# Routed block with 64 experts on one core: a fourth place for the down matrices, and three late shared tiles instead of four

## What is computed

```python
logits = xf @ w_router.T
top_vals, top_idx = jax.lax.top_k(logits, K)
w_tok = jax.nn.softmax(top_vals.astype(jnp.float32), axis=-1)
...
x_ec = xf[tok_ec]                                   # 64 experts x 64 places
g = jax.nn.silu(jnp.einsum('ech,ehi->eci', x_ec, w_gate))
u = jnp.einsum('ech,ehi->eci', x_ec, w_up)
y = jnp.einsum('eci,eih->ech', g * u, w_down)
contrib = (y * w_ec[..., None]).reshape(-1, h)
combined = jnp.zeros_like(xf).at[tok_ec.reshape(-1)].add(contrib)
combined = combined + silu(xf @ w_sh_gate) * (xf @ w_sh_up) @ w_sh_down
```

## Time and profile before

| | us |
|---|---|
| median of 3 runs | 703.38 (702.91 to 703.41) |
| the profiled execution | 701.8 |
| its span, first to last instruction | 699.9 |
| PE busy in the span | 661.4 (94%) |
| DVE, ACT, POOL busy | 316.3, 162.2, 220.5 |
| DMA packets | 203.17 MB, mean 290 GB/s over the span |

### The profile page before, as it was taken

How to read it: one execution, slowest core, us unless ns; L and a number is a source line. 1 busy time by engine, 2 the same in 40 slices (tenths; PEclk the granted TensorE clock), 3 DMA queues, 4 the chain that set the end, 5 groups by cost and what they waited for, 6 DMA issues and landing times.

```text
span 699.9 us, 8785 instructions
## 1 busy us (share of the span) xinstructions
PE 661.4 (94%) x3165; PEld 390.3 (56%) x3165; DVE 316.3 (45%) x750; ACT 162.2 (23%) x267; POOL 220.5 (32%) x209
## 2 busy tenths in 40 slices
PE   4999999999999898999999999999999999999873
PEld 3687878888878654444444444454454454444331
DVE  6887567759968771332332322233232222323111
ACT  5922215623211411121211211111121111112110
POOL 5537446446648131021222112221220203221011
PEclk9999999999999999999999999999999999999998
DMA  8201016713785979599999999999999999999993
GB/s 319 79 23 38 1 31 198 271 58 119 273 307 195 358 260 351 197 367 388 387 405 404 387 370 387 390 400 399 359 398 393 403 357 398 390 398 394 371 344 46
DMA packets 53195, 203.17 MB, mean 290 GB/s; under 512 B 7829, under 2 KB 8213, under 8 KB 52768
## 3 DMA queue, kind: packets, MB, share of 16 engines
q1 hardware_dynamic: 37360, 169.80, 61.3%
q0 software_dynamic: 8928, 21.26, 12.7%
q10 hardware_dynamic: 6864, 11.54, 4.4%
HBM read 179.21 MB, written 23.60 MB: 290 GB/s over the span
## 4 chain that ended last, share of the span: by engine, by line
PE 79%; DVE 5%; DMA 4%; issue 2%; ACT 1%; POOL 1%; POOLq 0%; SPq 0%; ACTq 0%; DVEq 0%
PE bank L1609 23%; PE bank L1394 13%; PE bank L1630 11%; PE bank L1527 9%; PE bank L1546 5%; PE bank L1416 4%; DMA extra<-in_L_ffn_w_up 3%; PE bank L1554 2%; PE bank L1441 2%; PE bank L1617 2%; PE bank L1539 1%; PE bank L1431 1%; PE bank L1583 1%; DVE key L1096 1%; PE bank L1363 1%
## 5 line engine op out<-in xcount | busy, mean ns | idle before, releaser
L652 POOL DMA_INDIRECT out_dram<-ym,midx x32 | 51.3, 1602 | 298.5 <-DVE ym L1260 107.1
L1609 PE MATMUL bank<-w_sb,xT 128*64 128x384 f32 x768 | 131.2, 494 | 2.8 <-issue 2.0
L1394 PE MATMUL bank<-x_hi,w_parts 128*128 128x512 f32 x368 | 114.9, 394 | 2.7 <-DVE x_lo L991 2.2
L1609 PEld LDWEIGHTS bank<-w_sb,xT 128*64 128x64 f32 x768 | 53.5, 138 | 74.3 <-issue 69.9
L1630 PE MATMUL bank<-w_sb,guT 128*64 128x512 f32 x384 | 88.0, 593 | 4.4 <-issue 4.4
L1394 PEld LDWEIGHTS bank<-x_hi,w_parts 128*128 128x128 f32 x368 | 69.6, 190 | 18.5 <-DVE x_lo L991 3.0
L1195 DVE TENSOR_TENSOR gu<-sg,bank 128x384 f32<-128x384 f32 x32 | 17.7, 555 | 126.1 <-PE bank L1609 65.2
L1394 PE MATMUL bank<-x_lo,w_parts 128*128 128x512 f32 x184 | 70.9, 394 | 0.0
L1527 PE MATMUL bank<-sh_sb,xS 128*128 128x384 f32 x192 | 63.9, 486 | 0.0
L1630 PEld LDWEIGHTS bank<-w_sb,guT 128*64 128x64 f32 x384 | 27.7, 137 | 53.3 <-issue 52.6
L1527 PEld LDWEIGHTS bank<-sh_sb,xS 128*128 128x128 f32 x192 | 35.7, 191 | 22.3
(11 more groups left out here) (187 smaller groups left out, 917.8 us busy)
## 6 DMA issues: line engine op xcount, KB each, us to landing
w_sb<-in_L_ffn_w_down SPq DMA_DIRECT2D x64, 768.0 KB
w_sb<-in_L_ffn_w_gate SPq DMA_DIRECT2D x48, 768.0 KB
w_sb<-in_L_ffn_w_up SPq DMA_DIRECT2D x48, 768.0 KB
extra<-in_L_ffn_w_gate SPq DMA_DIRECT2D x16, 768.0 KB
extra<-in_L_ffn_w_up SPq DMA_DIRECT2D x16, 768.0 KB
ring<-in_L_attn_x SPq DMA_DIRECT2D x14, 256.0 KB, 3.9
xt_dram<-xwT ACTq DMA_DIRECT2D x12, 256.0 KB, 2.9
xS<-xt_dram SPq DMA_DIRECT2D x12, 256.0 KB
```

Source lines behind the costliest of these rows:

```text
L652: pool.indirect_dma_start(out=out[:, :], out_offset=bass.IndirectOffsetOnAxis(ap=midx[j % 3][u][:, :], axis=0), in_=ym[u][:, :], in_offset ...
L1394: ins = pe.matmul(ps[u][:, :], w, xp, start=(n == 0), stop=(n == len(parts) - 1))
L1609: ins = pe.matmul(ps[e * C:(e + 1) * C, 0:I], xT[:, c, e * C:(e + 1) * C], gate_up(2 * j + u, e, k)[:, c, :], start=(c == 0), stop=(c == K ...
```

## The change

`place` is p mod 4 for all three kinds of matrix, so the down matrices have four places too. The room for the fourth comes from writing the gated rows over `sg` (no `gu` tiles any more; ACT's silu now waits for the transposes of the rows ahead instead of for their product), from moving `yS` onto the residual rows of the late tiles, and from moving `ym1` and `last_tok`. `load_down(p)` waits for the down product four pairs earlier, and SP's order becomes gate of p, up of p, down of p - 1; the down matrices of pair 3 are loaded ahead of group 0, one expert's right behind gate and up of pair 3, the other's after the late products. LEAD is 3 and FIRST is 1: three late tiles, all made ahead of group 0; group 0 has no shared product (it keeps the down product of the third late tile), and 13 tiles run in the groups 1 to 13. Tile 12 is therefore stored to DRAM by ACT, both as residual and transposed, ahead of group 0. BATCHES becomes 3, 6, 9, 12 and 13, the last with one tile. Ahead of group 0 the transposes of the third late tile go before the down product of the second.

```diff
-LEAD = 4
+LEAD = 3
 TAIL = 3
...
-FIRST = 2
+FIRST = 1
...
-            return p % (SLOTS + 1 if k < 2 else SLOTS)
+            return p % (SLOTS + 1)
...
-        BATCHES = range(FIRST + 2, FIRST + SHARED, 3)
+        BATCHES = [*range(FIRST + 2, FIRST + SHARED, 3), FIRST + SHARED - 1]
+
+        def batch(j):
+            last = j - FIRST
+            return last // 3 * 3, last + 1
...
             def load_down(p):
 
-                sp.wait_ge(d_ready[(p - SLOTS) % 2], (p - SLOTS) // 2 + 1)
+                sp.wait_ge(d_ready[p % 2], p // 2 - 1)
                 fill_matrix(sp, p, 2)
...
             fill_matrix(sp, 3, 0)
-            sp.wait_ge(u_ready[2], 1)
             fill_matrix(sp, 3, 1, (1,))
+            fill_matrix(sp, 3, 2, (1,))
             sp.wait_ge(half_ready, 1)
...
             fill_matrix(sp, 3, 1, (0,))
+            sp.wait_ge(u_ready[2], LEAD)
+            fill_matrix(sp, 3, 2, (0,))
             for p in range(4, 2 * GROUPS):
-                if p > 4:
-                    load_down(p - 2)
                 if p % 2 and 2 <= (p - 1) // 2 - FIRST < SHARED:
                     load_shared_tile((p - 1) // 2 - FIRST)
                 for k in range(2):
                     load_matrix(p, k)
-            load_down(2 * GROUPS - 2)
+                if p > 4:
+                    load_down(p - 1)
             load_down(2 * GROUPS - 1)
...
-                    pool.dma_start(out[(j - FIRST - 2) * P:(j - FIRST + 1) * P, :].rearrange("(a p) m -> p a m", p=P),
-                                   yS[:, :, :], accum_op=ALU.add).then_inc(added, ADD)
+                    t0, t1 = batch(j)
+                    pool.dma_start(out[t0 * P:t1 * P, :].rearrange("(a p) m -> p a m", p=P),
+                                   yS[:, 0:t1 - t0, :], accum_op=ALU.add).then_inc(added, ADD)
...
             def shared_out(t):
 
                 act.wait_ge(d_ready[2], t + LEAD + 1)
+                if t == 0:
+                    act.wait_ge(late_stored, 16 * LEAD)
...
-                dve.tensor_tensor(gu[0][:, :], sg[0][:, :], ps_u[0][:, 0:I], ALU.mult).then_inc(gu_ready[u], 1)
+                dve.tensor_tensor(sg[0][:, :], sg[0][:, :], ps_u[0][:, 0:I], ALU.mult).then_inc(gu_ready[u], 1)
...
             late_product(2, 1)
+            turn_shared(2, ps_xt)
             down_shared(1)
-            turn_shared(2, ps_xt)
...
                     down_shared(TAIL - 1)
-                    for w in range(2):
-                        late_product(TAIL, w)
```

More of the change, by code:

```diff
@@ L191, in moe_block @@
         assert 4 * ROW * 4 + W * 4 + 2 * 2048 <= 2 * KC * D * 4 + 2 * D * 4
-        sg, gu = ([tile(f"{name}{n}", [P, I], at=None if n < 1 else xw_at + i * I * 4) for n in range(2)]
-                  for i, name in enumerate(("sg", "gu")))
+        sg = [tile(f"sg{n}", [P, I], at=None if n < 1 else xw_at) for n in range(2)]
         guT = [tile(f"guT{n}", [P, IC, P], at=None if n < 1 else st_at + 2048) for n in range(2)]
         y, y_low = tile("y", [P, D], F32R, at=ramp_at), tile("y_low", [P, D], F32R, at=logits_at)
-        ym = [tile(f"ym{u}", [P, D]) for u in range(2)]
+        ym = [tile(f"ym{u}", [P, D], at=None if u < 1 else xw_at + I * 4) for u in range(2)]
         same = [tile(f"same{u}", [P, P], F32R) for u in range(2)]
@@ L201, in moe_block @@
         other_tok = [tile(f"other_tok{i}", [P, n * C], F16, at=a)
[L202 to L208, removed]
+                     for i, (n, a) in enumerate(((16, key_at), (8, wo_at + 2 * KC * D * 4 + 2 * D * 4 - 1024), (8, xw_at + I * 4 + 2048)))]
+        last_tok = tile("last_tok", [P, P], F16, at=st_at + 2048 + I * 4)
+        late_at = inv_at + (LATE - TILES) * 2048
+        yS = tile("yS", [P, 3, D], at=late_at)
+        assert st_at == vx_at + K4 and late_at + 3 * 2048 == out_at
+        extra_at = late_at - 2 * W * 4
+        assert top[0] <= extra_at - W * 4
+        assert 16 * C * 2 <= (HALF + C) * 4
         extra = [[tile(f"extra{k}{e}", [P, W], at=a) for e, a in enumerate(places)]
-                 for k, places in enumerate(((extra_at, extra_at + W * 4), (xin_at, wo_at + 4 * ROW * 4)))]
+                 for k, places in enumerate(((extra_at, extra_at + W * 4), (xin_at, wo_at + 4 * ROW * 4), (vx_at, extra_at - W * 4)))]
         assert W * 4 <= 3 * 2048
@@ L218, in place @@
         def place(p, k):
-            return p % (SLOTS + 1 if k < 2 else SLOTS)
+            return p % (SLOTS + 1)
         def uses(p, k):
-            return p // (SLOTS + 1 if k < 2 else SLOTS)
+            return p // (SLOTS + 1)
         def matrix(p, e, k):
@@ L234, in has_shared @@
         def has_shared(j):
-            return j == 0 or FIRST <= j < FIRST + SHARED
+            return FIRST <= j < FIRST + SHARED
         def item(j):
-            return LEAD + j - FIRST if j else TAIL
+            return LEAD + j - FIRST
         def in_parts(j, u):
@@ L333, in moe_block @@
         tok_ready, tok_turned, idx_ready = sem("tok_ready"), sem("tok_turned"), sem("idx_ready")
-        w_full = [[sem(f"w_full{k}_{i}") for i in range(SLOTS + (k < 2))] for k in range(3)]
+        w_full = [[sem(f"w_full{k}_{i}") for i in range(SLOTS + 1)] for k in range(3)]
         xg_full = [sem2(f"xg_full{r}") for r in range(2)]
@@ L882, in silu @@
                 act.wait_ge(g_ready[u], j + 1)
-                need(act, gu_ready[1 - u], j + u)
+                need(act, gu_turned[1 - u], j + u)
                 act.activation(sg[0][:, :], ps_g[0][:, 0:I], ACT.Silu).then_inc(sg_ready[u], 1)
@@ L887, in silu_shared @@
                 act.wait_ge(g_ready[2], t + 1)
-                need(act, gu_ready[2], t)
+                need(act, gu_turned[2], t)
                 act.activation(sg[1][:, :], ps_g[1][:, 0:I], ACT.Silu).then_inc(sg_ready[2], 1)
@@ L921, in group @@
                     pair_out(j, 1)
-                if first:
-                    store_late(TAIL)
-                elif shared:
+                if shared:
                     shared_out(j - FIRST)
@@ L1205, in gated_shared @@
                 need(dve, gu_turned[2], t)
-                dve.tensor_tensor(gu[1][:, :], sg[1][:, :], ps_u[1][:, 0:I], ALU.mult).then_inc(gu_ready[2], 1)
+                dve.tensor_tensor(sg[1][:, :], sg[1][:, :], ps_u[1][:, 0:I], ALU.mult).then_inc(gu_ready[2], 1)
             def turn_copy_shared(t):
@@ L1319, in group @@
                 merged_out(j, 0)
-                if first:
-                    shared_residual(TAIL)
                 same_tokens(j, 1)
@@ L1538, in turn_shared @@
                 for c in range(IC):
-                    ins = pe.transpose(ps[:, c * P:(c + 1) * P], chunk(gu[1][:, :], c, IC), ident[:, :])
+                    ins = pe.transpose(ps[:, c * P:(c + 1) * P], chunk(sg[1][:, :], c, IC), ident[:, :])
                 ins.then_inc(gu_turned[2], 1)
@@ L1616, in turn_gated @@
                 for c in range(IC):
-                    ins = pe.transpose(ps_ht[:, c * P:(c + 1) * P], chunk(gu[0][:, :], c, IC), ident[:, :])
+                    ins = pe.transpose(ps_ht[:, c * P:(c + 1) * P], chunk(sg[0][:, :], c, IC), ident[:, :])
                 ins.then_inc(gu_turned[u], 1)
```

## The result

| | before | changed |
|---|---|---|
| median of runs, us | 703.14 | 696.51 (696.30 to 696.61) |
| ratio, 95% interval | | 0.9908 (0.9896 to 0.9921) |
| profiled execution, us | 701.8 | 696.56 |
| its span, us | 699.9 | 694.7 |

The kernel is faster by 0.9%. The span fell by 5.2 us, where 4.9 were forecast. What follows is how the profile after says so, stage by stage.

What follows compares the result with a forecast made beforehand. PE and DMA both full, weights falling behind until PE starves at the end. DMA end 8.6 us earlier, PE start 1.1 later, but adds end the span at 695.0, 4.9 less: median 698.5 us, range 694.0 to 703.0.

Steps and rivals of the forecast that it cites:

- part 1: DMA around group 0: 9.9 us idle time won, 1.3 lost to new tile traffic; DMA end 8.6 us earlier.
- part 2: PE's work over the groups: same instructions, extra merged pair at most 0.3 us, silu's new wait harmless; zero change.
- part 3: PE's start of group 0: 1.1 us later, 0.8 from the first gather and 0.3 from the swap.
- part 4: Chain of adds from pair 24 on, with batches in groups 12 and 13: sets the span's end at 695.0 us.
- Rival C: Fifth batch costs what three tiles cost, or adds behind it stay slow: slower, 705 to 711 us; chance 0.10.
- Rival A: At the end, PE or the weights bind, not the adds: 694 to 696.5 us; chance 0.20.
- The sign that the last add wouldn't wait for `ym`: On POOL at the end: the last add not waiting for PE's `ym` would show the chain of adds binding.
- The last step, from span to median: Span gain of 4.9 us (699.9 to 695.0) taken off the median of 703.38, giving 698.5 us.
- B: First gather takes 9.0 to 10.4 us, PE starts 4.3 to 5.7 later: 701.7 to 703.1 us; chance 0.13.
- D: Idle time returns behind pair 5, leaving some 4 us of the DMA's gain: 701 to 703 us; chance 0.05.

Runs made afterwards that it cites:

- e3: Changed kernel with three places for down instead of four and SP's load order of before: median 698.37 us, ratio 0.9950.
- e4: Changed kernel without its fifth batch, so tile 12's shared result is not added (a probe, no usable kernel): median 690.96 us, ratio 0.9851.
- e8: Changed kernel with three down places, SP's load order of before and batches of 3, 3, 3, 2, 2: median 695.91 us, ratio 0.9914.
- e2: Kernel before with the fourth down place alone and the tile moves that make room for it: median 693.99 us, ratio 0.9890.
- e7: Kernel before with the fourth down place alone and its 12 shared tiles in batches of 3, 3, 2, 2, 2: median 692.19 us, ratio 0.9860.

## Why the prediction was right, and where a size was off

**The DMA's idle time (part 1).** Right in kind, 2 us too small. I took 9.9 us of idle time less 1.3 for the new tile, 8.6. The last packet of SP's queue ended at 672.9 us instead of 683.5, 10.6 us sooner, and e3, without the place, has it at 678.3. The rows show terms that I did not add, or took at their upper end. The 3.5 idle us of 255 to 260 took the first down matrix of pair 3 (share 1.03 now). Against them stand 2.5 us lost at 245 to 250 and 1.6 at 265 to 275. And the 1.3 for the new tile were too many: in the packets its accumulating store counts once (each of the three queues carried 0.26 MB more over the whole span), so 0.7 is what the bytes give. That makes 9.9 + 3.5 - 2.5 - 1.6 - 0.7 = 8.6, the sum that I had only because these terms cancel; the 10.1 us of weights carried by 290 us, less 0.7, say 9.4. What the remaining 1 to 2 us are, no run shows. SP's gate of pair 5 went out at 278.12; I had 278.

**PE's work (part 2).** Right: group 14 starts at 635.05 (634.60 before), though PE began 0.95 us later. The silu's new wait shows up once, ahead of group 0: at 247.21 ACT's idle time ends with the transposes (L1543), where before it ended with the product, at 246.42. It held PE up nowhere, and from group 0 on all of ACT's waits ahead of `sg` end with the products (L1613, L1531).

**The start (part 3).** 1.1 us forecast, 0.95 measured (265.56 against 264.61), in part by luck. I gave 0.8 to the gather and 0.3 to the swap. Both sizes were off: the swap costs 0.6 to 0.7 us, twice what I gave it, and the slower gather nothing beside it, since it landed 0.04 us ahead of the copy that PE had to wait for anyway. The other 0.4 us are the gather's later issue in this execution. The gather itself took 5.88 us, against 5.04 before, or 5.6 at most, as PE's start at 263.13 allows. The Trainium skill (DMA: Bandwidth & Descriptors, Queues, rings and completion order) has each DMA engine take turns between its queues. From it I had made that the weights would slow the first gather; at shares of 1.03 and 0.99 it lost 0.3 to 0.8 us, far from the 4 to 5 that the median and the maximum of all gathers would give. Why the later gathers take 9 us is not shown.

**The adds (part 4).** This decided the forecast, and the chain is the one forecast. Forecast and measured issue times on POOL, in us:

| | forecast | measured |
|---|---|---|
| pair 24 | 610.4 | 609.80 |
| batch in group 12 | 619.5 | 619.03 |
| pair 25 | 634.9 | 635.55 |
| pair 26 | 644.3 | 645.11 |
| fifth batch | 653.4 | 654.79 |
| pair 27 | 662.8 | 663.66 |
| pair 28 | 672.2 | 672.76 |
| pair 29 | 679.2 | 678.41 |
| pair 30 | 685.2 | 684.79 |
| pair 31 | 687.1 | 686.64 |
| end of the span | 695.0 | 694.7 |

No time is off by more than 1.4 us, but the links themselves are less exact, and their errors cancel. The batch of three took 16.5 us to the next add (15.4 forecast) and the wait ahead of the fifth batch 9.7 (9.1); the first add with the weights in took 5.65 (7). The 1.9 us from pair 30 to pair 31 stand in no row of before; 1.85 were measured. The one unknown, the price of a one-tile batch, was taken from the nearest row, an add of the same bytes: 9.4 forecast to the next add, 8.9 measured. Rival C (it costs like three) is refuted by the 7.94 us. Rival A (PE or the weights bind) describes e4 and e8, and not this kernel; the chain of waits tells this, and not the time, since the measured 696.51 lies just where A's 694 to 696.5 ends and the forecast's 696.5 to 701 begins. The sign that the last add wouldn't wait for `ym` is not plain in POOL's rows (pair 30's ends its idle time with a `ym` copy), but that copy had itself waited 3.08 us for an add. The Trainium skill's fit (DMA: Bandwidth & Descriptors, Anatomy of one DMA) gives 2.6, 3.2 and 3.8 us as estimates for one, two and three tiles; beside full engines they took 7.9, 11.4 to 12.3 and 14.3 to 15.5. An add of one tile's bytes took 4.75 us once the weights were in, so the load is a good part of the difference. The runs do not part the rest of it from the accumulating.

**The last step, from span to median.** The forecast of 698.5 was 2.0 us too high, with a span right to 0.3. The profiled execution of before, 701.8, lay 1.3 to 1.6 under its own median, and I took the gain off the median. A profiled execution takes its span plus 1.9 in both kernels; 695.0 + 1.9 = 696.9 would have been the better sum.

**Rivals B and D.** B (a gather of 9.0 us or more) is refuted by the 5.88 us of the changed kernel. D (the place doesn't bring what it is for) is refuted by the shares from 275 us on and by e2.

## What to carry to other kernels

When several resources are full at once, list for each the earliest end that it alone allows, and forecast the largest; a change that frees one lands on the next, here the chain of accumulating stores. Look at what a change does to the end of such a chain: the tile that moved from the late ones to the streamed ones cost a fifth store two groups from the end. The kernels without it have the shorter spans, and e7, which keeps the place and spreads the batches, is faster beyond the noise. Idle time of a streaming resource counts wherever it lies ahead of the full stretch: a megabyte carried 400 us earlier is 2.6 us off the end of the stream, though not off the kernel's, if another chain ends it.

## What was not expected of the hardware

- The price of an accumulating batch grows with its bytes, but less than in proportion: 7.9, 11.4 to 12.3 and 14.3 to 15.5 us for one, two and three tiles of 256 KB beside full DMA engines. An add of 256 KB takes 8.2 to 9.3 us beside them and 4.75 to 4.9 once the weights are in. With the 0.9 us to the next issue that is 9.1 against 5.65 us per link of the chain (pairs 27 to 29), 1.6 times as fast.
- The full stretch runs at 390 GB/s in the kernel before and 389 in the changed one, with deeper prefetch and more loads outstanding. The fourth place brought nothing there; it counted where the stream had paused.
